# A graph layer on one core: SyncE fetches a quarter of one edge group in each sixth round row by row, and its other loads are merged

## What is computed

```python
h = relu(layernorm(x))                                   # 12500 x 128
cat = concatenate((h[src], h[dst], edge_attr), axis=-1)  # 200000 x 384
msg = relu(cat @ W1 + b1)
aggr = segment_sum(msg, dst, 12500)
out = x + gamma * (t - mean(t)) / sqrt(var(t) + 1e-5) + beta   # t = aggr + h
```

## Time and profile before

| | |
|---|---|
| median of 3 runs | 1979.93 us (1979.79 to 1980.49) |
| the profiled execution | 1981.21 us |
| its span, first to last instruction | 1979.4 us |
| POOL busy | 1486.8 us |
| PE, ACT, DVE busy | 1568.1, 1315.3, 860.4 us |
| moved by DMA | 305.82 MB, mean 155 GB/s |
| granted TensorE clock, mean | 0.903 |

### The profile page before, as it was taken

How to read it: one execution, slowest core, us unless ns; L and a number is a source line. 1 busy time by engine, 2 the same in 40 slices (tenths; PEclk the granted TensorE clock), 3 DMA queues, 4 the chain that set the end, 5 groups by cost and what they waited for, 6 DMA issues and landing times.

```text
span 1979.4 us, 51290 instructions
## 1 busy us (share of the span) xinstructions
PE 1568.1 (79%) x11881; PEld 1485.0 (75%) x11881; DVE 860.4 (43%) x3031; ACT 1315.3 (66%) x2288; POOL 1486.8 (75%) x1575
## 2 busy tenths in 40 slices
PE   5677888878888887888888778888878787877876
PEld 4577787877777787777777777778777677777766
DVE  6534444444444444444444444444344343434434
ACT  5566767667676666767676676767666676666655
POOL 7777777777777777777777777777777777777775
PEclk9888988889898888998888899889899998999998
DMA  9744645555454555555555555555555555555553
GB/s 247 203 135 141 172 139 162 151 154 158 141 171 143 160 155 148 166 139 165 148 155 157 147 166 144 158 154 157 152 146 151 149 150 151 158 146 151 145 158 86
DMA packets 244448, 305.82 MB, mean 155 GB/s; under 512 B 50892, under 2 KB 143540, under 8 KB 244420
## 3 DMA queue, kind: packets, MB, share of 16 engines
q1 hardware_dynamic: 168596, 192.06, 31.9%
q0 software_dynamic: 50048, 102.60, 20.4%
q10 hardware_dynamic: 25776, 10.86, 1.9%
HBM read 281.68 MB, written 23.64 MB: 154 GB/s over the span
## 4 chain that ended last, share of the span: by engine, by line
POOL 30%; issue 23%; DMA 20%; PE 13%; DVEq 7%; DVE 4%; POOLq 1%; ACT 1%; ACTq 0%
POOL a_rows L524 27%; DMA a_rows<-table_a,picks 20%; DVEq L1225 5%; PE ps_pre L678 4%; PE ps_pre L679 4%; POOL aggr L500 3%; PE ps_edge L665 2%; DVE msg L1221 2%; PE ps_sum L690 1%; PE ps_sum L697 1%; DVEq L1218 1%; DVE e_norm L1253 1%; ACT space L894 0%; DVEq L1220 0%; PE ps_fin L690 0%
## 5 line engine op out<-in xcount | busy, mean ns | idle before, releaser
L524 POOL DMA_INDIRECT a_rows<-table_a,picks x1500 | 1417.1, 945 | 457.0 <-issue 402.5
L678 PE MATMUL ps_pre<-w_c,edge_cols 128*128 128x128 f32 x3128 | 680.6, 303 | 60.2 <-issue 39.6
L679 PE MATMUL ps_pre<-b_win,onehot_cols 128*128 128x128 f32 x3128 | 670.7, 300 | 0.0
L1221 DVE TENSOR_TENSOR msg<-ps_pre,a_rows 128x512 f32<-128x512 f32 x391 | 270.2, 691 | 874.1 <-DMA a_rows<-table_a,picks 640.3
L907 ACT ACTIVATE msg<-msg 128x512 f32<-128x512 f32 x391 | 246.2, 630 | 603.1 <-DVE msg L1221 587.0
L678 PEld LDWEIGHTS ps_pre<-w_c,edge_cols 128*128 128x128 f32 x3128 | 538.8, 216 | 83.5 <-ACT edge_cols L900 63.3
L679 PEld LDWEIGHTS ps_pre<-b_win,onehot_cols 128*128 128x128 f32 x3128 | 540.2, 216 | 0.0
L894 ACT ACTIVATE space<-space,base_all 64x512 f32<-64x512 int32 x391 | 474.1, 1213 | 13.3 <-issue 10.1
L690 PE MATMUL ps_sum<-onehot,msg 128*128 128x64 f32 x1568 | 225.2, 291 | 105.8 <-ACT e_rows L925 54.9
L690 PEld LDWEIGHTS ps_sum<-onehot,msg 128*128 128x128 f32 x1568 | 212.5, 210 | 125.0 <-ACT e_rows L925 65.5
L902 ACT ACTIVATE onehot_cols<-space,ones 64x512 f32<-64x512 f32 x391 | 277.4, 709 | 0.0
(11 more groups left out here) (123 smaller groups left out, 1032.8 us busy)
## 6 DMA issues: line engine op xcount, KB each, us to landing
edges<-in_edge_attr SPq DMA_DIRECT2D x391, 256.0 KB
space<-in_dst SPq DMA_DIRECT2D x391, 128.0 KB
a_rows<-table_a,picks POOLq DMA_INDIRECT x1500
b_win<-table_b SPq DMA_DIRECT2D x391, 32.0 KB
out<-out_rows SPq DMA_DIRECT2D x97, 64.0 KB
table_b<-b_rows ACTq DMA_DIRECT2D x96, 64.0 KB
x_all<-in_x SPq DMA_DIRECT2D x13, 448.0 KB, 6.8
table_a<-a_out SPq DMA_DIRECT2D x13, 448.0 KB
```

Source lines behind the costliest of these rows:

```text
L524: pool.indirect_dma_start(a_rows[:, u, k, :], None, table_a[:, :], bass.IndirectOffsetOnAxis(ap=picks[:, u, k:k + 1], axis=0),).then_inc(s ...
L678: pe.matmul(to, edge_cols[:, u % 2, k * P:(k + 1) * P], w_c[:, :], start=True, stop=False)
L679: mm = pe.matmul(to, onehot_cols[:, u % 2, k * P:(k + 1) * P], b_win[:, u, :], start=False, stop=True)
L1221: dve.tensor_tensor(msg[:, u % 2, :, :].rearrange("p k f -> p (k f)"), ps_pre[u % 2][:, :], a_rows[:, u, :, :].rearrange("p k f -> p (k f) ...
```

## The change

**POOL** leaves out one gather in each set of six rounds: quarter 3 of the first group of the sixth round. 16 of its 1500 gathers go.

**SP** fetches these 128 rows itself. The numbers come from `hand_picks`, 16 partitions of 128 integers, which DVE fills once during preparation from a new load of 32 KB. SP reads eight numbers into registers with one instruction and issues eight transfers of one row (512 bytes) each, into the new tile `hand_rows`. There are 16 such batches in a set: after the `b_win` of groups 1, 2 and 3 of the first five rounds, and after that of group 1 of the sixth.

**SP's other loads are merged.** Edges and receivers are loaded for two groups at once (`pair`), after both slots are free; the four least receivers of a round are read into registers by one instruction (`bases`), without the check; the `b_win` load stays one per group (`window`). SP's loop over a round becomes a loop over a set of six rounds, written out.

**DVE** adds that group in two instructions, quarters 0 to 2 with `a_rows` and quarter 3 with `hand_rows`, and waits for 128 rows before the second.

```diff
+PAIR = 2
+BATCH = 8
+HAND_K = SUB - 1
...
+            sp.dma_start(edges[0:EARLY_GROUPS, 0, :].bitcast(I32),
+                         src[0:EARLY_GROUPS * EARLY * UNROLL * GROUP].rearrange(
+                             "(s g e) -> s g e", s=EARLY_GROUPS, e=GROUP)[:, (EARLY - 1) * UNROLL, :]
+                         ).then_inc(s_hand_ids, 16)
...
-                    sp.dma_start(edges[:, u, :], group_rows(start_of(i, u))).then_inc(s_edges[u], 16)
...
-                    base = sp.value_load(base_i[0:1, bass.ds(g, 1)], min_val=0, max_val=N - 1)
...
+                def pair(i, h):
+                    g = i * UNROLL + h * PAIR
+                    if past(i, 1):
+                        sp.wait_ge(s_edge_turned, g - UNROLL + PAIR)
+                        sp.wait_ge(s_apart, g - UNROLL + PAIR)
+                    sp.sem_inc(s_gate_sp, 1)
+                    start = i * (UNROLL * GROUP) + h * (PAIR * GROUP)
+                    sp.dma_start(edges[:, h * PAIR:(h + 1) * PAIR, :], pair_rows(start)).then_inc(s_edges[h], 16)
+                    sp.dma_start(dst_win[:, h * PAIR:(h + 1) * PAIR, :].rearrange("w u e -> w (u e)"),
+                                 receivers_of(start, PAIR)).then_inc(s_dst_win[h], 16)
...
+                def bases(i):
+                    _, values = nc.values_load_multi_w_load_instructions(
+                        base_i[0:1, bass.ds(i * UNROLL, UNROLL)], [mybir.EngineType.SP], min_val=0, max_val=N - 1,
...
+                def window(i, u, base):
                     if u == 0:
                         sp.wait_ge(s_b_stored, 16 if isinstance(i, int) and i < 2 else (i - 1) * 16)
+                        sp.sem_inc(s_gate_sp, 1)
+                    if past(i, 1):
+                        sp.wait_ge(s_pre, (i - 1) * UNROLL + u + 1)
+                    sp.sem_inc(s_gate_sp, 1)
                     sp.dma_start(b_win[0:WIN, u, :], table_b[bass.ds(base, WIN), :]).then_inc(s_b_win[u], 16)
...
+                def fetch(s, j, u):
+                    batch = j * (UNROLL - 1) + u - 1
+                    if batch == P // BATCH - 1:
+                        pass
+                    elif u == 0 or batch >= P // BATCH:
+                        return
+                    if batch == 0 and past(s, 1):
+                        sp.wait_ge(s_z, (s * EARLY - 1) * UNROLL + 1)
+                        sp.sem_inc(s_gate_sp, 1)
...
+                    _, rows = nc.values_load_multi_w_load_instructions(
+                        numbers, [mybir.EngineType.SP], min_val=0, max_val=N - 1,
...
+                    for n in range(BATCH):
+                        p = batch * BATCH + n
+                        sp.dma_start(hand_rows[p:p + 1, :], table_a[bass.ds(rows[n], 1), :]).then_inc(s_hand_rows, 16)
+
+                def round_(i, s=None, j=None):
+                    base = bases(i)
+                    for u in range(UNROLL):
+                        if u % PAIR == 0:
+                            pair(i, u // PAIR)
+                        window(i, u, base[u])
+                        if s is not None:
+                            fetch(s, j, u)
+                    if past(i, 3):
+                        store(i - 3)
...
                     for u in range(UNROLL - 1):
-                        step(s * EARLY + EARLY - 1, u)
+                        step(s * EARLY + EARLY - 1, u, HAND_K if u == 0 else SUB)
...
+                        dve.tensor_tensor(msg[:, u % 2, 0:HAND_K, :].rearrange("p k f -> p (k f)"),
+                                          ps_pre[u % 2][:, 0:HAND_K * H],
+                                          a_rows[:, u, 0:HAND_K, :].rearrange("p k f -> p (k f)"), ALU.add)
+                        dve.wait_ge(s_hand_rows, handed * (P * 16))
+                        dve.tensor_tensor(msg[:, u % 2, HAND_K, :], ps_pre[u % 2][:, HAND_K * H:], hand_rows[:, :],
+                                          ALU.add).then_inc(s_z, 1)
```

More of the change, by code:

```diff
@@ L147, in build @@
         onehot = sb("onehot", [P, 4, SUB, P])
+        hand_ids = edges[0:EARLY_GROUPS, 0, :].bitcast(I32).rearrange("s (p k) -> s p k", k=SUB)
         edge_cols = sb("edge_cols", [P, 2, GROUP])
@@ L230, in build @@
         s_gate_dve = sem("s_gate_dve")
-        s_edges = [sem(f"s_edges{u}") for u in range(UNROLL)]
+        s_gate_sp = sem("s_gate_sp")
+        s_edges = [sem(f"s_edges{h}") for h in range(UNROLL // PAIR)]
         s_b_win = [sem(f"s_b_win{u}") for u in range(UNROLL)]
@@ L238, in build @@
         s_edge_turned = sem("s_edge_turned")
-        s_dst_win = [sem(f"s_dst_win{u}") for u in range(UNROLL)]
+        s_dst_win = [sem(f"s_dst_win{h}") for h in range(UNROLL // PAIR)]
         s_count_kept = sem("s_count_kept")
@@ L267, in build @@
         s_out_stored = sem("s_out_stored")
+        s_hand_ids = sem("s_hand_ids")
+        s_hand_picks = sem("s_hand_picks")
+        s_hand_rows = sem("s_hand_rows")
         s_first_picks = sem("s_first_picks")
@@ L313, in group_rows, with pair_rows, receivers_of @@
             return edge_attr[bass.ds(start, GROUP), :].rearrange("(p k) f -> p (k f)", p=P)
[L315 to L319, removed]
+        def pair_rows(start):
+            return edge_attr[bass.ds(start, PAIR * GROUP), :].rearrange("(g p k) f -> p g (k f)", p=P, k=SUB)
+        def receivers_of(start, groups):
+            return dst[bass.ds(start, groups * GROUP)].rearrange("(o e) -> o e", o=1).to_broadcast([WIN, groups * GROUP])
         def x_block(b):
@@ new lines, in tail @@
+                def tail():
+                    g = (ROUNDS - 1) * UNROLL + PAIR
+                    sp.wait_ge(s_edge_turned, g - UNROLL + 1)
+                    sp.wait_ge(s_apart, g - UNROLL + 1)
+                    sp.dma_start(edges[:, PAIR, :], group_rows(TAIL_START)).then_inc(s_edges[1], 16)
+                    sp.dma_start(dst_win[:, PAIR, :], receivers_of(TAIL_START, 1)).then_inc(s_dst_win[1], 16)
+                def bases(i):
+                    _, values = nc.values_load_multi_w_load_instructions(
+                        base_i[0:1, bass.ds(i * UNROLL, UNROLL)], [mybir.EngineType.SP], min_val=0, max_val=N - 1,
+                        skip_runtime_bounds_check_because="the least receiver of a group is a node")
+                    return values
@@ L424, in _, with store @@
[L424 to L435, removed]
+                def store(b):
+                    sp.wait_ge(s_out, b + 1)
+                    sp.dma_start(out[bass.ds(b * P, P), :], out_rows[:, 0, :]).then_inc(s_out_stored, 16)
@@ L444, in load_early @@
                                  ).then_inc(s_early_loaded, 16)
-                with sp.Fori(3, EARLY) as i:
-                    round_(i)
-                load_early(0)
+                def fetch(s, j, u):
[7 more added lines that the diff above has]
+                        sp.sem_inc(s_gate_sp, 1)
+                    if isinstance(s, int):
+                        numbers = hand_picks[s:s + 1, batch * BATCH:(batch + 1) * BATCH]
+                    else:
+                        numbers = bass.at_runtime_partition(hand_picks[0:1, batch * BATCH:(batch + 1) * BATCH], s)
+                    _, rows = nc.values_load_multi_w_load_instructions(
+                        numbers, [mybir.EngineType.SP], min_val=0, max_val=N - 1,
+                        skip_runtime_bounds_check_because="src holds node numbers")
+                    for n in range(BATCH):
+                        p = batch * BATCH + n
+                        sp.dma_start(hand_rows[p:p + 1, :], table_a[bass.ds(rows[n], 1), :]).then_inc(s_hand_rows, 16)
@@ new lines, in round_, with rounds @@
+                def round_(i, s=None, j=None):
[8 more added lines that the diff above has]
+                        store(i - 3)
+                def rounds(s):
+                    for j in range(EARLY):
+                        round_(s * EARLY + j, s, j)
+                    load_early(s)
@@ L449, in _ @@
+                sp.wait_ge(s_zero, 1)
+                for par in range(2):
+                    sp.wait_ge(s_a_stored[par], (CHUNKS // 2) * 16)
+                sp.wait_ge(s_b_first, 1)
+                sp.wait_ge(s_hand_picks, 1)
+                rounds(0)
                 with sp.Fori(1, EARLY_GROUPS) as s:
-                    with sp.Fori(0, EARLY) as j:
-                        round_(s * EARLY + j)
-                    load_early(s)
+                    rounds(s)
                 round_(ROUNDS - 2)
+                base = bases(ROUNDS - 1)
@@ L454, in _ @@
+                pair(ROUNDS - 1, 0)
                 for u in range(LEFT):
-                    step(ROUNDS - 1, u)
+                    if u == PAIR:
+                        tail()
+                    window(ROUNDS - 1, u, base[u])
                 for b in range(ROUNDS - 4, BLOCKS):
@@ L517, in _, with step @@
             with pool.If(crooked < 1):
-                def step(i, u):
+                def step(i, u, gathers=SUB):
                     pool.wait_ge(s_picks, i * UNROLL + u + 1)
```

(18 more changed lines are left out.)

21 lines of the change are left out of this document (7 added, 14 removed).

## The result

The change makes the kernel slower: 2042.69 us median (2040.68 to 2048.87), where the kernel before has 1979.86; ratio 1.0324, 95% interval 1.0311 to 1.0337. That is 63 us more; the forecast was 19 us less. It is rival 1 of the prediction, SyncE as the bound.

What follows compares the result with a forecast made beforehand. POOL was taken as the bound at 1.249 us a gather: 1979.9 less 20.0 for 16 gathers gives 1959.9, plus 1 us for edges, 1961 us. Range 1957 to 1966 for the forecast alone, up to 2165 with rival 1.

Steps and rivals of the forecast that it cites:

- rival 1: SyncE becomes the bound at L481 and L486 (numbers read singly, or dearer rows): slower, 2062 to 2425 us; chance 0.43.
- What bounds before, and what 16 gathers are worth: POOL is full over the whole loop; 16 gathers fewer at 1.249 us save 20.0 us.
- SyncE's account of a set: Sum of SyncE's work for six rounds: 113.5 us against the 113.7 that POOL's 91 gathers last.
- it fits: SyncE's new work just fits into a set, so POOL's gain is kept: 1957 to 1966 us; chance 0.47.
- 0.39 × 16 = 6.2: SyncE's 16 loads of eight numbers a set, each priced like a load of one number: 6.2 us.
- I take 0: Each number after the first in a register load costs nothing; the range was 0 to 35 us a set.
- I take 1: Instruction fetches for SyncE's longer written-out loop: 1 us a set, between bounds of 0 and 4.9.
- The 200 ns for each register: The skill's price for register loads from HBM, even in bulk: 26 us more a set, a time of 2374.
- 128 × 0.50 = 64.0: SyncE's 128 row fetches a set, each 0.50 us for address, move, issue and gap: 64.0 us.
- 4 windows = 3.0: SyncE's four window loads a round, each 0.25 wait and register operation, 0.47 issue, 0.04 gap: 3.0 us.
- Rival 3: Late edges or windows push the sums beyond their 6 us reserve; 1976 us at 1 us beyond; chance 0.03.
- 0.5, the gain is gone: Profile sign at register load L481: about 0.27 us expected, gain gone at 0.5, rival 1 in full at 1.8.

Runs made afterwards that it cites:

- e3: Changed kernel with only every second row of a batch fetched (64 of 128 a set), the others counted as zero; 1960.70 us, ratio 0.9903.
- e5: Changed kernel with SyncE's loop over the 15 later sets written out in full; 1960.09 us, ratio 0.9902.
- e1: Kernel before with the merged loads alone: all 1500 gathers stay with POOL, SyncE fetches no rows; 1980.53 us, ratio 1.0008.
- e7: Changed kernel with two sets in the loop's body instead of one, and one more set before the loop; 2016.97 us.
- e2: Changed kernel reading one number a batch instead of eight, all eight rows being that one row; 1960.41 us, ratio 0.9905.

## Why the prediction was wrong

- **What bounds before, and what 16 gathers are worth.** Right: e3 and e5 give 1960.7 and 1960.1 for the 1959.9 of the sum.
- **SyncE's account of a set.** Right in kind, wrong in size: 113.5 for 119.4, with a margin of 0.2 us. Forecasting "it fits" on that margin was the failing choice; rival 1 said it would turn slower from 0.011 us a number on. The terms missed by +7.8 (loads of numbers), +3.5 (windows), +2.1 (loads of bases), +1.6 (branch and early load), +0.2 (the rest) and −9.3 (rows).
- **The step "0.39 × 16 = 6.2" for the number loads.** It failed most: 14.0 measured. "I take 0" for further numbers was nearly right (0.036 each, 4.0 us a set). The rest, about 3.7 us in 10 of the 16 loads, is the first load behind rows, which neither the forecast nor rival 1 had. The load of bases missed the same (+2.1). Rival 1 was right in its sign and in its place. That its sum with 0.036 a number, 16 × (118.2 − 114.9) = +53, 2033 us, comes near 2043 is luck: rows too dear there make up for the loads behind rows, the windows and the branch.
- **The step "I take 1" for fetches.** A taken branch over the long body (677 instructions of SyncE) costs 3.2 us, 0.31 over the short one of e1 (260). It lay within the bound of 4.9. In the trace of the changed kernel a packet of q14 starts 1.4 to 1.9 us behind the start of each of the 14 taken branches, before the next instruction; in e7 one does behind each of its six; in e1 none falls between a branch and the next instruction. The Trainium skill ("Runtime: NRT & Kernel Launch", "Instruction fetch mechanics") says that a taken branch out of a window of two 16 KiB pages forces a fetch. The trace agrees: 124 packets of instructions on q14 where there were 19, and 20 in e1, whose loop has no rows in it. It also says that this is one reason why kernels prefer to be unrolled; e5 agrees with 13 us a set, of which the branch is only 3.2.
- **The 200 ns for each register.** The Trainium skill ("Runtime: NRT & Kernel Launch", same section) gives that figure for register loads that elsewhere on the page come from HBM. From SBUF the traces show 36 ns for a further number up to eight and 57 beyond, and the estimate of 2374 by that page was far off.
- **"128 × 0.50 = 64.0".** Too dear by 9.3 us: issue 225 ns instead of 286, and shorter register operations. It hid part of the other misses.
- **"4 windows = 3.0".** 3.6: left out were an operation for the gate semaphore ahead of each window (0.07 each) and, once a round, the wait for `table_b` with its own operation (0.14); an issue with its gap takes 0.55, not 0.51.
- **Rival 3,** late merged loads: e1 shows no cost; the waits of PE and ACT in the changed kernel follow from SyncE's lag, and in e5, with the same merged loads, ACT's are down from 455 us to 56.
- **What the profile should show:** the gaps before L587 came, and of the waits on `s_pre` 13.9 us are left of 507; L481 at "0.5, the gain is gone" was passed with 0.9. That sign was set too high by the prediction's own sum: 0.011 a number is a load of 0.35, and 0.5 would already be some 46 us of loss. PE's wait came at the edges and not at `b_win`, probably since edges are issued with the shorter lead.

## What to carry to other kernels

A queue engine that looks idle can be filled to the last microsecond by issuing transfers, and then its own control flow decides: written out, the same work costs SyncE some 106 us a set, and POOL bounds again; in a loop over 677 instructions it costs 119.4, with address arithmetic for most transfers and 3.2 us at every branch. Sum such a budget with every small instruction in it, register loads, semaphore operations and branches, and where the margin is under the error of the sum, forecast the range and not the floor. When an engine off the path gets work, first undo its loop and group its register loads ahead of its transfers.

## What the runs showed of the hardware that was not expected

- The first register load of SyncE behind a run of one-row fetches takes 0.2 to 0.4 us longer (0.28 or 0.65 us with one number in e2, 0.54 or 0.91 with eight), whether one, three or six other transfers stand in between, and after four rows (e3) as after 8 or 24; the next load doesn't. What it waits for, no row shows.
- A backward branch of SyncE took 0.18 us over a body of one round in the kernel before, 0.31 over a set without rows (e1) and, in the changed kernel, 2.9 to 3.4 over a set with rows, with an instruction packet of q14 in each of these last pauses.
- The issue of a one-row transfer takes 225 ns, less than the 286 of L360's and half of the 469 of a 64-row window.
